# The weighted sums of the two expert layers: ScalarE weights the second answers, VectorE adds them four tiles at a time

## The reference, cut to what matters

```
x = x + mamba(layernorm(x));            x = x + cross_attention(layernorm(x), ctx)
x = x + experts_L0(layernorm(x))        # 8 experts, top 2, gelu
x = x + self_attention(layernorm(x));   x = x + cross_attention(layernorm(x), ctx)
x = x + experts_L1(layernorm(x))        # 8 experts, top 2, gated with silu
```

## Time and profile before

| | us |
|---|---|
| median of 3 runs | 1562.05 |
| the 3 runs | 1555.59 to 1565.16 |
| the profiled execution, whole | 1557.63 |
| its span in the trace | 1555.9 |
| VectorE busy in the span | 1038.8 (67%) |
| ScalarE busy | 888.5 (57%) |
| TensorE busy (matmuls) | 1192.1 (77%) |

### The profile page before, as it was taken

One profiled execution on the slowest core, in us unless ns is written; L12 is line 12 of the kernel. 1 busy time (PEld: TensorE's weight loads), 2 busy tenths in 40 slices (PEclk: granted clock), 3 DMA queues, 4 the chain that ended last, 5 costly groups with the idle time before them and its releaser, 6 DMA issues. The chain is left out here.

```text
span 1555.9 us, 31340 instructions
## 1 busy us (share of the span) xinstructions
PE 1192.1 (77%) x11216; PEld 925.2 (59%) x11216; DVE 1038.8 (67%) x2380; ACT 888.5 (57%) x1657; POOL 813.9 (52%) x654
## 2 busy tenths in 40 slices
PE   5789789789877588888459992699966999727991
PEld 2566666567666346666359992366643666627991
DVE  2999999999899667887501114477634799733445
ACT  4777877877875168776135550377733766503440
POOL 1887887887785421656735551211001256684661
PEclk9999999999999799897579996699986999958996
DMA  5202203203200230101167775300014001127875
GB/s 190 84 28 111 84 28 111 84 28 111 83 28 1 58 56 9 37 26 42 57 205 225 227 216 162 65 9 16 16 24 109 9 28 35 44 90 212 253 239 164
DMA packets 98157, 140.09 MB, mean 90 GB/s; under 512 B 13709, under 2 KB 77242, under 8 KB 93716
## 3 DMA queue, kind: packets, MB, share of 16 engines
q1 hardware_dynamic: 86708, 120.41, 25.4%
q0 software_dynamic: 9088, 17.07, 3.2%
q10 hardware_dynamic: 2208, 0.61, 0.2%
HBM read 107.52 MB, written 28.16 MB: 87 GB/s over the span
## 5 line engine op out<-in xcount | busy, mean ns | idle before, releaser
L318 POOL TENSOR_TENSOR M_dbx<-M_u,M_b_sb 128x1024 f32<-128x1024 f32 x128 | 299.7, 2359 | 57.5 <-DVE M_h L377 56.8
L377 DVE TENSOR_TENSOR_SCAN M_h<-M_pA,M_dbx 128x512 f32<-128x512 f32 x256 | 297.4, 1201 | 6.2 <-POOL M_dbx L318 5.0
L530 ACT ACTIVATE M_pA<-M_dt,M_a_neg 128x504 f32<-128x504 f32 x256 | 174.7, 683 | 47.6 <-DVE M_h L377 43.0
L540 ACT ACTIVATE M_hc<-M_pT,M_cT 128x256 f32<-128x256 f32 x256 | 119.1, 466 | 59.7 <-PE M_pT L670 58.0
L2359 PE MATMUL X_bank<-F_xT,F_wbuf 128*128 128x256 f32 x624 | 150.2, 384 | 0.0
L670 PE MATMUL M_pT<-M_ident,M_h 128*128 128x128 f32 x512 | 85.0, 291 | 79.7 <-ACT M_hc L540 45.8
L2019 POOL DMA_INDIRECT F_slots<-F_line,F_pos x128 | 127.0, 992 | 36.0 <-issue 35.8
L686 PE MATMUL M_pY<-M_ident,M_hc 128*128 128x128 f32 x1024 | 140.7, 282 | 0.0
L670 PEld LDWEIGHTS M_pT<-M_ident,M_h 128*128 128x128 f32 x512 | 59.4, 147 | 131.7 <-DVE M_h L377 68.6
L686 PEld LDWEIGHTS M_pY<-M_ident,M_hc 128*128 128x128 f32 x1024 | 131.6, 200 | 1.1
L1615 ACT ACTIVATE X_pt_sb<-X_bank 128x512 f32<-128x512 f32 x128 | 76.3, 596 | 86.2 <-PE X_bank L1747 86.2
(11 more groups left out here) (322 smaller groups left out, 2760.3 us busy)
## 6 DMA issues: line engine op xcount, KB each, us to landing
M_b_sb<-M_rows_bc SPq DMA_DIRECT2D x32, 1024.0 KB, 4.8
F_wbuf<-in_F_wcat SPq DMA_DIRECT2D x39, 578.0 KB, 4.0
F_wbuf<-in_F_wcat SPq DMA_DIRECT2D x39, 450.0 KB, 4.1
X_s_sb<-F_slots SPq DMA_DIRECT2D x39, 132.0 KB, 3.8
F_xblk<-F_slots SPq DMA_DIRECT2D x39, 132.0 KB, 3.9
F_line<-F_line SPq DMA_DIRECT2D x16, 256.0 KB, 2.7
X_kT<-F_answers SPq DMA_DIRECT2D x8, 512.0 KB, 5.7
X_kv<-in_ctxT SPq DMA_DIRECT2D x2, 1344.0 KB, 10.3
```

Of the source, the lines that this page charges most:

```text
L318: pool.tensor_tensor(dbx[:, k % DBXS, :, :], u[:, g % 2, :, :], bc(b_sb[:, n, :], 1, 2), ALU.mult).then_inc(dbx_ready, 1)
L377: v.tensor_tensor_scan(h[:, k % STATES, half, :], pA[:, (2 * k + half) % DECAYS, :, :].rearrange("p b t -> p (b t)"), dbx[:, k % DBXS, hal ...
L530: act.activation(pA[:, (2 * k + half) % DECAYS, :, 1:SEQ], dt[:, g % 2, half, :].rearrange("p (b t) -> p b t", t=SEQ)[:, :, 1:SEQ], ACT.Ex ...
L540: act.activation(hc[:, k % SCALED, t, :], pT[:, 0, t, :], ACT.Identity, scale=cT[:, g % 2, t, n:n + 1]).then_inc(hc_ready, 1)
```

## The change

`vector_sum` keeps the first half: four SCALAR_TENSOR_TENSOR operations that add the weighted first answers to x, and the `link` behind them. The second half is split. A new function `scalar_weigh` on ScalarE, run behind `scalar_blocks`, waits for `weight_ready` once and for `ya_in[g]` of each group, and multiplies the four second answers of the group in place by their weights, with four Identity activations of 128x128 whose `scale` is a per-partition pointer. The fourth raises a new semaphore `second_ready`. VectorE waits for it and then adds all four tiles of second answers to x in one TENSOR_TENSOR of 128x512, which raises `sum_done`. SP's stream, the loads and the stores are as they were. Both layers use the functions.

```diff
     def vector_sum(v, link, g, weight):
         v.wait_ge(ya_in[g], 16)
-        for k in range(2):
-            for t in range(TILES):
-                n = g * TILES + t
-                ins = v.scalar_tensor_tensor(x[:, n, :], ya(g)[:, t, k, :], weight[:, n, k:k + 1], x[:, n, :],
-                                             ALU.mult, ALU.add)
-            if k == 0:
-                link(ins)
-        ins.then_inc(sum_done, 1)
+        for t in range(TILES):
+            n = g * TILES + t
+            ins = v.scalar_tensor_tensor(x[:, n, :], ya(g)[:, t, 0, :], weight[:, n, 0:1], x[:, n, :],
+                                         ALU.mult, ALU.add)
+        link(ins)
+        v.wait_ge(second_ready, g + 1)
+        xs = x[:, g * TILES:(g + 1) * TILES, :]
+        v.tensor_tensor(xs, ya(g)[:, :, 1, :], xs, ALU.add).then_inc(sum_done, 1)
+
+    def scalar_weigh(act, g, weight):
+        act.wait_ge(ya_in[g], 16)
+        for t in range(TILES):
+            n = g * TILES + t
+            ins = act.activation(ya(g)[:, t, 1, :], ya(g)[:, t, 1, :], ACT.Identity, scale=weight[:, n, 1:2])
+        ins.then_inc(second_ready, 1)
+
+    st.scalar_weigh = scalar_weigh
...
             d.scalar_exp(act)
             f.scalar_blocks(act)
+            act.wait_ge(d.weight_ready, 1)
+            for g in range(GROUPS):
+                f.scalar_weigh(act, g, d.weight)
```

More of the change, by code:

```diff
@@ L2226, in expert_stage @@
     ya_in = [m.sem(f"ya_in{i}") for i in range(GROUPS)]
-    sum_done = m.sem("sum_done")
+    sum_done, second_ready = m.sem("sum_done"), m.sem("second_ready")
     st.sum_done = sum_done
```

## The result

The changed kernel takes 1558.09 us (median of 20 runs, 1547.4 to 1562.75) where the kernel before takes 1563.59 us (20 runs, 1555.59 to 1571.12). The ratio is 0.9962 with a 95% interval of 0.9947 to 0.9978: 5.9 us less, between 3.4 and 8.3. The ratios and intervals of this document are worked out over the runs without those in the kernel's slower state, and differ a little from the quotients of the medians (which lie 5.5 us apart here). The forecast was 0.45% less, 7.0 us. Timed twice more, on other chips, the ratio was 0.9972 (0.9948 to 0.9995) and 0.9977 (0.9938 to 1.0016).

What follows compares the result with a forecast made beforehand. VectorE, not the transfers, was taken to set both tails' pace. Per layer, 8 x 0.45 - 0.1 = 3.5 us, 7.0 for both, from 1557.63 to 1550.6; plus 4.4 for a median, 1555.1 us (0.45% less), range 1549.0 to 1561.5.

Steps and rivals of the forecast that it cites:

- VectorE's first half, 1.18 us: In both expert layers' tails: four kept operations and the wait for the fourth, 1.15 + 0.03 = 1.18 us a group.
- The addition, 0.68 us, 0.60 from start to start: VectorE's new 128x512 addition in each tail group: 0.60 us from start to start, at most 1.13.
- 0.45 us a group: VectorE's saving in each tail group: second half's 1.05 us less the addition's 0.60; 3.6 us a layer over eight groups.
- ScalarE, 1.1 to 1.2 us a group, a wait of 0.1 us once: ScalarE's four weightings take 1.1 to 1.2 us a tail group; VectorE waits 0.1 us in group 0 only.
- Loads in time: In the tails, nobody waits for loads at the new pace, by 0.6 us at the nearest.
- The stores, nothing charged: At each tail's end, the last store lands 2.3 us after issue, just behind the transfers' floor; charged nothing.
- the floor lies 0.3 to 0.4 us below: just not reached: Earliest landing of each tail's last store at 346 GB/s: 968.2 against 968.5 in layer 0, 1549.7 against 1550.1 in layer 1.
- The sum, 3.5 us a tail: Saving in each layer's tail: 8 x 0.45 - 0.1 = 3.5 us, 7.0 us for both.
- The clock's moment: Rival: TensorE's clock rise behind layer 0's tail stays fixed in time, losing 1.75 us; median 1556.8, chance 0.13.
- ScalarE's pace: Rival: weightings at 0.61 us make ScalarE need 2.44 us a tail group, 4.8 us more in all; 1566.9, chance 0.06.
- a dear addition: Rival: VectorE's tail addition takes 1.05 us from start to start, so nothing is gained; about 1562, chance 0.06.
- Transfers taking 1.2 us of each tail: Rival: 1.2 us of backlog before each layer's last store, gain 2.3 us each, 4.6 in all; 1557.5, chance 0.13.

Runs made afterwards that it cites:

- the run with four additions: Changed kernel with the one 128x512 addition taken apart into four of 128x128; tails 24.82 and 24.9 us, against 23.16 and 23.2 for the changed kernel.
- first answers alone: Changed kernel without the second answers' weighting and addition, loads and stores as they were; tails 23.23 and 23.3 us.
- bfloat16 in layer 1: Changed kernel with layer 1's expert answers written, loaded and read as bfloat16; tails 23.17 and 22.0 us, ratio to the kernel before 0.9948.
- ScalarE weighting both: Changed kernel with ScalarE weighting both answers, eight activations a group, and VectorE adding 128x512 twice; tails 29.08 and 29.6 us.
- with GpSimd: Changed kernel with bfloat16 answers in layer 1 and GpSimd making the 128x512 addition there; layer 1's tail 29.5 us, ratio to the kernel before 0.9996.
- changed again: The changed kernel itself, timed again beside the kernel before; median 1558.72 us against 1564.34, ratio 0.9972, tails 23.28 and 23.3 us.

## Why the prediction was right, step by step

- **VectorE's first half, 1.18 us:** 1.14 + 0.03 measured. Right.
- **The addition, 0.68 us, 0.60 from start to start:** 0.69 and 0.61. It was taken from a row with one source in PSUM and held for two in SBUF beside transfers at 346 GB/s. The Trainium skill's VectorE: DVE Perf Modes, section on the TRN2 errata, gives (N + 151) / 0.96 ns for a float32 tensor_tensor, an estimated 691 ns for 512; the measured mean is 692.
- **0.45 us a group:** 2.23 to 1.78. Right, and the run with four additions splits it nearly in halves.
- **ScalarE, 1.1 to 1.2 us a group, a wait of 0.1 us once:** 1.28 us and 0.22. The term was too small by 0.1 us, since 0.36 us for one weighting was 0.39 and 0.25 from start to start was 0.29. The line through 504 and 256 elements gives too little at 128; whether that is a fixed part of a short activation or the writing in place wasn't tried. No table load shows in the tail.
- **Loads in time:** right. VectorE waits for none but the first. ScalarE starts on group 4 10.9 us behind the first load (10.8 forecast).
- **The stores, nothing charged:** in layer 0 the last store landed 2.5 us behind its issue and not 2.3; in layer 1 it was 2.3. The step "the floor lies 0.3 to 0.4 us below: just not reached" was off by just this margin: with all of the second half taken off VectorE the tail doesn't shorten. The mechanism was named, its distance was mis-sized, and the total suffered little because the floor and VectorE came out at the same moment; that is partly luck. The forecast's floor was 968.2 - 947.47 = 20.7 us from the first load to the last landing, eight stores in a row at the full rate; measured with VectorE out of the way it is 21.2. Layer 1 of that kernel says where the 0.5 us lie: store 0 lands at 1661.8, 15.2 us behind the first load, just as in the earlier trace rows (1536.5 + 7.9 - 1529.2), and the last one at 1667.6, 5.8 us later. The forecast's term for these seven stores was 5.3 us, 0.76 each; it measured 0.83. Why they land further apart than the rate gives wasn't tried.
- **The sum, 3.5 us a tail:** 3.3 and 3.5. The parts separate it: the sums gave 3.4 in both, 0.1 less than forecast by ScalarE's wait. In layer 0 the end took 0.2 us of it and the first landing came 0.1 us earlier, in layer 1 the end came 0.1 us earlier; differences of 0.1 us there also stand between executions of the same kernel.
- **The clock's moment:** the rise moves with the work. Windows in the self attention phase of the changed kernel and of the one with first answers alone, to be laid beside the earlier trace rows, and one of the kernel with bfloat16 in layer 1:

```profile
1003.00:1005.00 2.00, 2.00 (x3) 0.67 (x3) 0.00 (x0) 0.00 (x0) 0.00 (x0) 0.50 0.00 0
1005.00:1007.00 2.00, 2.00 (x22) 1.15 (x21) 0.14 (x1) 1.10 (x2) 0.00 (x0) 1.00 0.00 0
```

```profile
1040.00:1042.00 2.00, 2.00 (x10) 0.84 (x3) 1.31 (x3) 0.00 (x0) 0.00 (x0) 0.50 0.00 0
1042.00:1044.00 2.00, 2.00 (x5) 0.86 (x4) 1.18 (x2) 0.00 (x0) 0.00 (x0) 0.81 0.00 0
```

```profile
993.00:996.00 3.00, 1.57 (x3) 0.34 (x1) 0.45 (x2) 2.74 (x5) 0.00 (x0) 0.82 0.87 151
```

  From the phase's first load it is 25 us before (973.9 to 999), 25 us changed (979.8 to 1005), 22 to 23 us in the third (1020.2 to 1043) and only 13 in the fourth (980.95 to about 994). Over all thirteen profiles it is 22 to 26 us in ten and 13 to 14 in three (four additions, ScalarE weighting both, bfloat16 in layer 1). So it isn't bound to a moment of the program, and it isn't a fixed distance behind the phase's start either. What picks the early rise these runs don't show. Its price they do: the kernels with bfloat16 in layer 1, without and with GpSimd, do the same work from the self attention's first load to the second tail, and take 548.35 us with the early rise and 554.51 with the late one, 6.2 us apart; before, changed and changed again, all with the late one, lie between 554.6 and 555.3. That is as much as the whole gain, it is a part of the spread, and no part of the change: before and changed both rise at 25 us.
- **The other rivals:** ScalarE's pace and a dear addition are refuted by the rows above. Transfers taking 1.2 us of each tail are refuted in size: they took 0.2 in layer 0 and nothing in layer 1.
- **Base:** the forecast stood on a median of three runs, 1562.05; over 20 it was 1563.59. The measured 1558.09 is 3.0 us above the forecast, half of it this; of the other half 0.3 us are the tails, and the rest is less than the interval.

## What to carry to other kernels

Before an engine's work in a stage is cut, add up the bytes that the stage moves and divide by the rate that its own windows show: here 6.3 MB at 346 GB/s stood so near to VectorE's 18 us that the first 3.4 us off VectorE were paid out and nothing behind them was. On short tiles half of such a gain can come from fewer instructions and half from moving work to an idle engine; keep the helper's work behind something that the main engine has to do anyway, and check the helper's pace against that of a group, not against one instruction. Where a change is smaller than the clock's spread of the whole, measure the stage from one fixed instruction to another.

## What the runs showed of the hardware that was not expected

- A VectorE operation with two SBUF sources lasted 1346 ns instead of 340 beside a GpSimd addition of 1.30 us in SBUF. ScalarE beside VectorE at the same tile cost nothing: 0.69 us for the addition with it and without it.
- Identity with a pointer scale on 128x128 float32 in place takes 0.39 us, 0.29 us from start to start.
- In the one kernel where GpSimd worked last, the program ended 9.6 us behind the issue of the last store (1552.9 to 1562.5), where behind VectorE it is 4.6 us (1553.6 to 1558.2).
- While loads in rows of 512 B ran, the transfers were at 308 GB/s; with loads in rows of 1 KB at 345 to 352. Stores alone, in rows of 512 B too, ran at 346 GB/s behind those loads (1009 to 1011), so it isn't the length of the row alone; that it is the loads' rows is argued and has no run of its own.
- The rise of TensorE's granted clock from 0.50 to 1.00 in one and the same phase came 13 to 14 us behind its first load in three executions and 22 to 26 in ten, and was worth 6.2 us in the one pair of executions with the same work.
